# Planner numbers, PSUM bank pairs, two direct plane moves and halved steps in the prologue of a decoder layer kernel

## The reference, cut to what matters

```python
# x: (2, 1024, 256); ctx: (2, 77, 256)
K = 2 * Re(sum_n Ct[h,n] * exp(dtA[h,n] * l))            # S4D kernel, l = 0..1023
y = irfft(rfft(x, 2048) * rfft(K, 2048))[:1024]          # long convolution per channel
r = x + y + x * D
x = LN(x + LN(r) * ln_w + ln_b)                          # stage 1
x = LN(x + MHA(q=x, k=ctx, v=ctx))                       # 16 heads of 16, 77 keys
x = LN(x + MLP(x) + product_key_experts(x))              # 1024 wide MLP, 1024 experts
```

## Time and profile before

| what | us |
|---|---|
| median of three runs (689.98 to 695.78) | 693.98 |
| the profiled execution | 689.71 |
| its span in the trace | 687.9 |
| head up to the end of the last taps matmul | 0 to 119.4 |
| spectra, products, inverse | 119.4 to 165.8 |
| PE idle for the last planes | 165.8 to 176.9 |
| convolution, first norms, queries, to the first score subtraction | 176.9 to 201.2 |
| attention of the first tiles, with the other norms | 201.2 to 269 |
| attention and feed-forward | 269 to 688 |

### The profile page before, as it was taken

How to read it: one execution, slowest core, us unless ns; L and a number is a source line. 1 busy time by engine, 2 the same in 40 slices (tenths; PEclk the granted TensorE clock), 3 DMA queues, 4 the chain that set the end, 5 groups by cost and what they waited for, 6 DMA issues and landing times.

```text
span 687.9 us, 9791 instructions
## 1 busy us (share of the span) xinstructions
PE 599.0 (87%) x3200; PEld 393.4 (57%) x3200; DVE 484.3 (70%) x955; ACT 403.9 (59%) x595; POOL 308.5 (45%) x354
## 2 busy tenths in 40 slices
PE   6809588795769598999999999999999999899896
PEld 2503477573636364454776745578565478453485
DVE  7976475662346885897857789765779796678782
ACT  3865446222143265996673878773778774677760
POOL 3704975554142456352263632243735243744441
PEclk9858879899695677999999999999999999999999
DMA  8994020368161000000000000000000000000000
GB/s 272 309 235 90 1 76 27 101 171 224 27 247 59 1 1 1 0 2 0 1 0 1 17 8 9 0 1 1 8 16 1 9 1 1 9 15 9 0 9 23
DMA packets 19613, 34.14 MB, mean 50 GB/s; under 512 B 7273, under 2 KB 13931, under 8 KB 18219
## 3 DMA queue, kind: packets, MB, share of 16 engines
q1 hardware_dynamic: 15179, 29.33, 14.8%
q10 hardware_dynamic: 4384, 4.20, 1.9%
HBM read 21.81 MB, written 10.65 MB: 47 GB/s over the span
## 4 chain that ended last, share of the span: by engine, by line
PE 64%; DVE 12%; DMA 6%; ACT 6%; POOL 6%; issue 5%; SPq 1%; DVEq 0%; POOLq 0%; ACTq 0%
PE banks L804 20%; PE banks L894 8%; PE banks L899 8%; PE banks L849 4%; PE banks L871 4%; PE banks L826 3%; DMA scr_x<-arena 3%; PE banks L861 3%; PE banks L679 2%; PE banks L746 2%; PE banks L835 2%; DMA scr_v<-arena 2%; PE banks L886 2%; DVE stats L1437 2%; PE banks L716 1%
## 5 line engine op out<-in xcount | busy, mean ns | idle before, releaser
L1260 POOL TENSOR_TENSOR arena<-arena 128x1024 f32<-128x1024 f32 x64 | 123.3, 1927 | 159.1 <-ACT arena L1122 158.3
L804 PE MATMUL banks<-arena 128*128 128x512 f32 x384 | 174.4, 596 | 5.3 <-issue 3.7
L804 PEld LDWEIGHTS banks<-arena 128*128 128x128 f32 x384 | 69.8, 190 | 83.0 <-issue 76.9
L1122 ACT ACTIVATE arena<-arena 128x1024 f32<-128x1024 f32 x64 | 73.5, 1149 | 7.5 <-DVE arena L1525 3.0
L1124 ACT ACTIVATE arena<-arena 128x1024 f32<-128x1024 f32 x64 | 73.5, 1149 | 2.1
L1525 DVE SCALAR_TENSOR_TENSOR arena<-arena 128x1024 f32<-128x1024 f32 x48 | 63.9, 1331 | 1.7
L1012 ACT COPY arena<-banks 128x512 f32<-128x512 f32 (+1 forms) x64 | 34.1, 532 | 46.2 <-PE banks L796 30.3
L894 PE MATMUL banks<-arena 128*128 128x256 f32 x256 | 58.4, 381 | 2.4 <-DVE arena L1547 2.2
L1233 POOL TENSOR_SCALAR arena<-mv 128x1 f32<-128x1 f32 (+1 forms) x40 | 14.4, 361 | 102.1 <-DVE mv L1438 100.7
L899 PE MATMUL banks<-arena 128*128 128x256 f32 x256 | 57.9, 379 | 0.0
L1026 ACT ACTIVATE tok<-tok,arena,rstd 128x256 f32<-128x256 f32 x48 | 27.9, 598 | 44.0 <-POOL arena L1238 43.0
(11 more groups left out here) (179 smaller groups left out, 1096.3 us busy)
## 6 DMA issues: line engine op xcount, KB each, us to landing
scr_x<-arena SPq DMA_DIRECT2D x16, 256.0 KB, 8.9
arena<-scr_x SPq DMA_DIRECT2D x4, 1024.0 KB, 11.0
scr_z<-arena ACTq DMA_DIRECT2D x14, 256.0 KB, 3.8
tok<-in_x SPq DMA_DIRECT2D x8, 256.0 KB, 6.1
arena<-scr_z SPq DMA_DIRECT2D x4, 512.0 KB
out<-tok SPq DMA_DIRECT2D x16, 128.0 KB, 1.7
arena<-scr_z SPq DMA_DIRECT2D x2, 640.0 KB
arena<-in_imat SPq DMA_DIRECT2D x1, 1152.0 KB, 5.5
```

Of the source, the lines that this page charges most:

```text
L804: ins = mm(bk[:, :], w[:, k, P * m:P * m + P], src[:, k, :], start=(k == 0), stop=(k == KC - 1))
L1122: fn(ebuf[m % 2], sxb[m % 2], ACT.Prelu, bias=negt[:, n % 2, h:h + 1], alpha=FAR).then_inc(s_ranked, 1)
L1260: tt(sxb[m % 2], sim[:, n % 2, h, 0:XR].unsqueeze(2).broadcast_to((P, XR, NKEYS)), sim[:, n % 2, FH + h, :].unsqueeze(1).broadcast_to((P, ...
```

## The change

All of it lies before the steady part; the steps of the steady part keep their order.

* `x_bias` moves from between POOL's tables to behind all its `spectra`; `values` moves to between tables 7 and the second `skip`; `keys` on DVE to directly behind tables 7, ahead of `spectra`; ACT's `stage` behind `sines(1)`.
* `taps` and `x_second` are interleaved on PE and ACT, and the bank pair now alternates over the merged list (`PAIR_AT`). A step waits for the evacuation of the step two places before it in that list (`pair_free`). PE's and ACT's order becomes: x_second 0, 1, 2, taps 0, x_second 3, taps 1, x_second 4, 5, taps 2, x_second 6, taps 3, x_second 7, 8, taps 4, then (PE) k_first 0, taps 5, k_first 1, k_first 2, taps 6, k_first 3, taps 7. The steps x_second 0, 2, 3, 4, 8 and taps 2, 3, 5, 7 use banks 4 and 5, the others 0 and 1; so taps 0 and taps 1 share a pair.
* The last two planes' steps (n = 16 and 17, three planes) go from `zring` straight into `zB` by three moves of 128 KB inside SBUF, issued on ACT's queue; the second half has three batches left.
* `conv` is cut in two: for q = 0..5 the part of the first channel half runs as soon as the planes of that half are there and all evacuations of planes are done; q = 3, 4, 5 use banks 4, 0 and 1 for it (`CONV_APART`). q = 6, 7 run as before.
* The first group's queries are made in halves of 256 tokens: turn1 0, queries of half 0, score 0.0, conv 7, score 0.1, turn1 1, queries of half 1. ACT's order there: queries of half 0, norm1 1, conv 7, turn1 1, score 0.0's exponential, a query, score 0.1's exponential, a query. DVE takes score 0.0 and 0.1 back to back, and `ln` 3 ahead of `residual` 2.

```diff
-Z_BATCHES = ((0, 1, 2), (3, 4), (5, 6), (7, 8))
+Z_BATCHES = (((0, 1, 2), (3, 4), (5, 6), (7, 8)), ((0, 1, 2), (3, 4), (5, 6)))
+Z_DIRECT = (FREQ + 7, FREQ + 8)
+CONV_EARLY = (0, 1, 2, 3, 4, 5)
+CONV_APART = {3: 4, 4: 0, 5: 1}
...
+         "query_first": (-0.08, -0.07, 0.245, 0.2684), "score_first": (0.0, 0.043), "turn2": (-0.001, 0.0655),
-         "taps": (0.982,), "x_second": (-2.2, 0.237), "skip": (1.3, 0.3), "k_first": (5.915, 0.66, 9.6, 0.247),
-         "simw": (-2.4,), "x_bias": (-0.466, 0.617), "values": (-1.576,), "stage": (-2.515,), "keys": (9.738,),
+         "taps": (1.261,), "x_second": (-0.5, 0.7), "skip": (1.248, 0.3), "k_first": (5.915, 0.66, 9.6, 0.247),
+         "simw": (-2.4,), "x_bias": (12.0, 0.1), "values": (7.2,), "stage": (-2.151,), "keys": (7.496,),
...
+        PAIR_USERS = [y for y in order(HEAD, "pe") if y[0] in ("taps", "x_second")]
+        PAIR_AT = {y: i for i, y in enumerate(PAIR_USERS)}
...
+        def pair_bank(kind, n):
+            return 4 * ((PAIR_AT[kind, n] + 1) % 2)
+
+        def pair_free(kind, n):
+            at = PAIR_AT[kind, n]
+            if at < 2:
+                return (s_xae, 2 * NQ) if at else (s_kbz, 1)
+            last, k = PAIR_USERS[at - 2]
+            return (s_kev, 2 * k + 2) if last == "taps" else (s_xfe, k + 1)
...
-                if g >= 2:
-                    pe.wait_ge(s_kev, 2 * g - 2)
-                b0 = group_bank(g)
+                pe.wait_ge(*pair_free("taps", g))
+                b0 = pair_bank("taps", g)
...
-                    if n == 0:
-                        pe.wait_ge(s_kbz, 1)
-                        pe.wait_ge(s_xfe, FREQ)
                     taps(n)
...
+            def conv_part(q, hf):
+                bk = conv_bank(q)[:, :].rearrange("p (b f n) -> p f b n", b=B, f=2)
+                for h in range(2):
+                    ins = mm(bk[:, hf], fai[:, h, :], zB[:, hf, h, q, :].rearrange("p (b n) -> p b n", b=B),
+                             start=(h == 0), stop=(h == 1), skip_group_check=True)
+                return ins
...
+                pe.wait_ge(s_zr[1], 16 * z_loads(1))
+                if q not in CONV_EARLY:
+                    w_unit(("conv", q, "a"))
+                    conv_part(q, 0)
+                conv_part(q, 1).then_inc(s_wmm, 1)
+
+            pe.wait_ge(s_late, 16 * 4)
+            pe.wait_ge(s_kev, 2 * NGRP)
+            pe.wait_ge(s_kae, 2 * QUAD)
+            pe.wait_ge(s_cross, 2 * FREQ)
+            pe.wait_ge(s_ze, 2 * FREQ)
+            pe.wait_ge(s_zr[0], 16 * z_loads(0))
+            for q in CONV_EARLY:
+                conv_part(q, 0)
...
-                    act.dma_start(t["scr_z"][hf, tiles[0]:tiles[0] + planes].rearrange("r p n -> p r n"),
-                                  zring[:, d, 0:planes]).then_inc(s_zw[d], 16)
+                    if n in Z_DIRECT:
+                        for j, r in enumerate(tiles):
+                            act.dma_start(zB[NS * r:NS * r + NS, hf].rearrange("p h q n -> p (h q) n"),
+                                          zring[:, d, j, :]).then_inc(s_zr[hf], 16)
+                    else:
+                        act.dma_start(t["scr_z"][hf, tiles[0]:tiles[0] + planes].rearrange("r p n -> p r n"),
+                                      zring[:, d, 0:planes]).then_inc(s_zw[d], 16)
...
-                    fn(qT[:, j, :], src, ACT.Identity, bias=pcol[:, j:j + 1]).then_inc(s_wact, 1)
+                    fn(qT[:, j, query_cols(step)], src[:, query_cols(step)], ACT.Identity,
+                       bias=pcol[:, j:j + 1]).then_inc(s_wact, 1)
```

More of the change, by code:

```diff
@@ L55 @@
 PAIRS = [(0, NC)] + [(2 * m - 1, 2 * m) for m in range(1, FREQ - 1)] + [(NC - 1,)]
[L58 to L65, removed]
-         "taps": (0.982,), "x_second": (-2.2, 0.237), "skip": (1.3, 0.3), "k_first": (5.915, 0.66, 9.6, 0.247),
-         "simw": (-2.4,), "x_bias": (-0.466, 0.617), "values": (-1.576,), "stage": (-2.515,), "keys": (9.738,),
+PLACE = {"probs": (0.166, 0.2592, 0.441), "score": (0.273, 0.6341), "attend": (0.592,), "turno": (0.772,),
+         "project": (1.4,), "project_last": (0.934,), "turn1": (-0.087, 0.0432), "query": (0.245, 0.2685),
+         "query_first": (-0.08, -0.07, 0.245, 0.2684), "score_first": (0.0, 0.043), "turn2": (-0.001, 0.0655),
+         "sim": (0.379,), "sim_first": (0.031,), "best": (0.432,), "best_first": (0.207,),
+         "pair": (0.283, 0.3903, 0.7922, 0.8026), "total": (0.847,), "first": (-0.1,), "sums": (-0.805,),
+         "exps": (-0.131,), "late": (-0.027, 0.0082, 0.7012),
+         "conv": (-2.338, -1.7115, -1.497, -1.4195, -1.329, -1.2905, -1.172, -0.9595),
+         "ln": (-1.672, -1.4035, 0.316, 1.2245, 1.9406, 2.373, 3.035, 3.1435),
+         "ln_steps": (-0.501, -0.234, 0.162, 0.013, 0.361), "sines": (-2.943, -2.336), "tables": (0.152,),
+         "taps": (1.261,), "x_second": (-0.5, 0.7), "skip": (1.248, 0.3), "k_first": (5.915, 0.66, 9.6, 0.247),
+         "simw": (-2.4,), "x_bias": (12.0, 0.1), "values": (7.2,), "stage": (-2.151,), "keys": (7.496,),
@@ L119, in queries @@
             for j in range(2):
-                put(start, kind, s, j, j=j)
+                if kind == "query" and s == 0:
+                    for half in range(2):
+                        put(start, kind, s, j, half, key="query_first", j=2 * half + j)
+                else:
+                    put(start, kind, s, j, j=j)
     def normed(at, tl, k):
@@ L483, in build @@
                 key = step + (part_,)
+                if step[0] == "conv" and step[1] in CONV_APART:
+                    wide_count += 1
+                    CONV_DONE[step[1]] = (s_wmm, wide_count)
+                    continue
                 W_AT[key] = len(W_FREE)
@@ L497, in w_bank, with query_of, query_cols, conv_bank @@
             return bank[5 + u % 3]
+        def query_of(tl, hh):
+            return ("query", 0, hh, tl // 2) if tl < SUPER else ("query", tl // SUPER, hh)
+        def query_cols(step):
+            return slice(W // 2 * step[3], W // 2 * (step[3] + 1)) if step[1] == 0 else slice(0, W)
+        def conv_bank(q):
+            return bank[CONV_APART[q]] if q in CONV_APART else w_bank(W_AT[("conv", q, "a")])
         def spectrum_of_x(m, hf):
@@ L520, in taps_bank, with z_loads @@
             return bank[(4 if hf else 6) + g % 2]
+        def z_loads(hf):
+            return len(Z_BATCHES[hf]) + sum(len(tiles_of(n % FREQ)) for n in Z_DIRECT if n // FREQ == hf)
         def z_writes(upto, d):
@@ L610, in _ @@
             for hf in range(2):
-                for batch in Z_BATCHES:
+                for batch in Z_BATCHES[hf]:
                     for n in (FREQ * hf + k for k in batch):
@@ L616, in _ @@
                                  t["scr_z"][hf, r0:r1].rearrange("r (s c) n -> (r s) (c n)", s=NS)).then_inc(s_zr[hf], 16)
-            sp.wait_ge(s_wmm, max(W_DONE[W_AT[("conv", q, "a")]][1] for q in range(NQ)))
+            sp.wait_ge(s_wmm, max((CONV_DONE[q] if q in CONV_APART else W_DONE[W_AT[("conv", q, "a")]])[1] for q in range(NQ)))
             for dst, n in ((dn, "dn"), (wg, "wg"), (wu, "wu"), (wd, "wd"), (up, "up")):
@@ L842, in _ @@
                         pe.wait_ge(s_vbd, 1)
+                        pe.wait_ge(s_wact, max(ACT_TURN[("conv", q, "a")] for q in CONV_APART if CONV_APART[q] == 4))
                     for c in range(PCH):
@@ L910, in evac_taps @@
             g, half = divmod(i, 2)
[L911 removed]
+            src = bank[pair_bank("taps", g) + half][:, :].rearrange("p (k c) -> p c k", c=P)
             ch = CH * (g % HALF_GROUPS) + HC // 2 * half
```

52 lines of the change are left out of this document (18 added, 34 removed).

## The result

| what | us |
|---|---|
| kernel before, median of four runs (689.98 to 695.78) | 694.05 |
| changed kernel, median of four runs (670.55 to 673.4) | 671.67 |
| ratio, 95% interval | 0.9699 (0.9665 to 0.9734) |
| profiled executions, before and after | 689.71, 673.4 |
| their spans | 687.9, 671.6 |

The account below looks back on a forecast made before the run. Bound before 269 us by x's round trip, POOL's queue delaying taps 0, the planes' wait and serial first tiles; gains 15.0 + 0.5 + 10.5 = 26.0 off the 694.0 median gave 668.0 us, range 658 to 678.

Parts of the forecast that it names:

- The rival that the handovers are hidden: Tap groups: the tables pace the groups, not the handovers of banks; gain 32.4, time 661.6 us, chance 0.10.
- the clock rival: Tap groups: PE loses its clock between the mixed steps, costing 5.3; gain 20.7, time 673.3 us, chance 0.14.
- the rival that the head does nothing: Tap groups: something else than POOL holds taps 0; gain only 10.5, time 683.5 us, chance 0.03.
- the forecast's chain: Tap groups: taps 0 from 58.9, then waits for evacuations, taps 7 done at 104.5 instead of 119.45; gain 15.0.
- of 64 (groups 0 and 4) 4.26: Tap groups: price of a taps group of 64 matmuls at full clock, 4.26 us, against 2.13 for 32.
- the bound of 109: Tap groups: the forecast counts as wrong if taps 7 ends after 109 or before 100 us.
- Spectra: Phase of 46.4 us after the last taps: moving `keys` out of its middle gains 0.5, between 0 and 4.1.
- Planes: Before the convolution's second half: direct moves take 6.6, all planes there at 173.9 on the old axis, bounds 173.0 and 177.
- the bound of "no gain": Planes: upper bound on their arrival, 177 on the old axis, where the direct moves gain nothing.
- The rival of slow direct moves: Planes: at half rate three take 9.7, arriving at 177.2, no earlier than before; gain 22.7, time 671.3 us, chance 0.13.
- First tiles: Planes' arrival to DVE's first score: 17.5 instead of 24.3, gain 6.8; then a loss of 0.8 to the first `probs`.
- The better clock from `probs` on and the earlier `ln`: Behind the first `probs`: gain taken as 1.5, between nothing and 4 us for the clock and the `ln`.

Follow-up runs that it names:

- e2_pool_back: Changed kernel with `values` and `x_bias` put back at POOL's head, as before the change: 687.84 us, ratio to the kernel before 1.001.
- e5_keys_back: Changed kernel with `keys` put back between spectra 5 and 6 on DVE: 674.33 us, 1.75 above the changed kernel run beside it.
- e12_one_direct: Changed kernel with only the last plane moved directly and the two planes of step 16 sent through DRAM: 673.26 us.
- e6_conv_whole: Changed kernel with the convolution in one piece for all eight slices, without early parts: 671.57 us.
- e4_queries_whole: Changed kernel with the first group's queries in one piece each, behind both transposes: 680.62 us, ratio 0.987 to the kernel before.
- e9_taps_first: Changed kernel with x_second 7 and 8 moved behind all taps and k_first 0 to 3 given new places: 673.58 us.
- c1_after: The changed kernel run again without edits, as yardstick of the third set: 672.14 us, ratio 0.9738 to the kernel before.
- e1_planes_back: Changed kernel with the three direct plane moves undone, the last planes going through DRAM again: 670.10 us.

## Why the prediction was right or wrong

**Direction and mechanism of the head: right.** POOL's queue held taps 0; with it gone, taps follow the handovers of banks. POOL adds at 52.9 (forecast near 54), PE waits for ACT before taps 1 and 3, and e2_pool_back shows that nothing of the gain is left without it. The rival that the handovers are hidden is refuted by the waits of 1.0 to 1.5 us, the clock rival by the window of the whole stretch, in which the granted clock is 1.00, the higher of the two levels, with PE busy 43 of 52 us, and the rival that the head does nothing by 11.2 us.

```profile
60.00:112.00 52.00, 43.08 (x646) 32.56 (x644) 38.15 (x33) 34.55 (x82) 33.89 (x19) 1.00 0.22 60
```

**Its size: 15.0 was 11.2, a sum with four mis-sized terms.** Measured against the forecast's chain, the first taps began 1.1 us late (60.01 for 58.9; x's round trip ended 1.4 later in this execution, 52.38 against 50.98). The term "of 64 (groups 0 and 4) 4.26" was worked out by doubling 2.13; it is 5.03, twice on the chain, 1.5 us. The trace of before holds both such groups, partly at the lower clock (0.50 in 74 to 76, 0.76 over 95 to 102), and I had not read them:

```profile
71.71 6.57 PE L679 MATMUL banks<-arena 64*128 64x128 f32 x64 [2.56 <-POOL arena L1204]
...
95.36 6.59 PE L679 MATMUL banks<-arena 64*128 64x128 f32 x64 [2.11 <-DVE arena L1397]
```

From taps 3's end to taps 4's start it took 5.0 instead of 4.4: the chain had taps 4 start once x_second 7 was evacuated, but x_second 8 stands ahead of it on PE, waits for the evacuation of taps 3 and lasts 1.90. And the last v add took 2.91 for 2.35, 0.6. Smaller differences cancel; it makes 3.8: taps 7 end at 108.28 instead of 104.5, just inside the bound of 109.

**POOL and PE's order aren't additive.** I gave the 15 us to one chain and did not ask what each half gives alone. The runs do: 2.8 and -4.1 (in those two traces and the changed kernel's, x's trip ended 1.2 to 1.4 later than in that of before, so each could stand 1 us better).

**`keys` beside POOL: a cost that I left out.** I put `keys` under the last taps and priced only what it frees. It slows POOL there, and POOL slows it. A row of the kernel before showed it already, and I had not read it: beside `keys` at 134.29 POOL's products took 1.30 and 1.16, a little earlier 0.73.

```profile
133.45 0.73 POOL L1147 TENSOR_TENSOR arena<-arena 128x256 f32<-128x256 f32 x1
134.39 1.30 POOL L1146 TENSOR_TENSOR arena<-arena 128x256 f32<-128x256 f32 x1 [0.21 <-DVE arena L1413]
```

`keys` reads both operands from SBUF (`arena`, `head_mask`); the tables' products read one from PSUM (`banks`), and beside them POOL's adds keep 2.35. The Trainium skill (SBUF — State Buffer, SBUF: two separate sides) has the rule: a VectorE operation with two SBUF inputs and a GpSimd operation that reads SBUF share a pair of ports, which one of them holds for its whole instruction. The rows of `keys` agree with it in that both engines slow down (6.01 for `keys`, 4.08 for `values`, 2.91 for the add). They do not show that one waits the other out: from 102.98 to 108.99 work was done that alone takes about 8.0 us, by my estimate (4.13 of `keys`, 2.35 of the add, some 1.5 of `values`). No run here sets the ports apart from another cause.

**Spectra: 0.5 was 2.0.** I took PE for the bound because it was busy 8.19 of 9.00 us. All the same the stretch is 0.5 to 2.0 shorter in the ten traces with `keys` gone from it (e5_keys_back has the comparison).

**Planes: the step that failed.** "I take 6.6, and all planes are there" 6.7 us after the last evacuation; it was 11.8, beyond the 8 that I had set as the point where the forecast is wrong, and beyond the bound of "no gain". My nearest row was four moves that together took 4.55 and fill 32 partitions each; this move fills 8. The rival of slow direct moves held, which had the planes 10.0 us after the last evacuation; it is 1.8 more, so that they come later than through DRAM. The lower bound failed too: the last batch that SP reads was to land 4.87 after its issue, and took 10.86. The Trainium skill (DMA: Bandwidth & Descriptors, Why a DMA increments its semaphore by 16 and not by 1) had the sign: fewer of the 16 engines for such a shape. But half the rate is not the whole of it, since one move took as long as three (e12_one_direct): 12.0 us from the last evacuation for one, 11.8 for three. By the rival's own working, 9.7 for three, one would have taken 3.2.

**First tiles: 6.8 was 4.9, and 0.8 was 1.4.** Conv's second parts began at 1.2 GHz (granted clock 0.57 in 166 to 170, 1.00 from there on), behind 4.45 us in which PE did nothing (forecast under 3), and DVE's first statistics (169.19) came 2.8 us after the planes instead of 1.6. That is 1.2; the half queries took 3.7 for 3.4, and the transposes and copies ahead of them 0.4 more. That the queries would be at the lower level was right (0.50 over their 3.7 us). The early parts of conv, which I had counted with 1.4 us and as cover, are worth nothing (e6_conv_whole). The better clock from `probs` on and the earlier `ln`, which I had at 1.5 together, gave 2.2: `probs` takes 1.09 where it took 1.97. Without the halves the clock is lost, and they are worth 6 by the traces and 8 by the medians (e4_queries_whole).

**The level.** The sum was 26.0 against 16.2 in the traces, yet the time was only 3.7 off. That closeness is luck in good part, and comes from the two executions: before's profiled one lay 4.3 below its median, the changed kernel's 1.7 above. It is luck too that the slow moves' rival gave 671.3, next to the 671.67 measured: it had the planes 3.3 us later than the forecast, where they were 5.1 later, and nothing of the head's 3.8. The three medians' gains of 22.4, 19.4 and 18.0 say that the sum was too large by 4 to 8 us.

## What to carry to other kernels

When a queue's delay and another engine's order hide each other, price each edit alone as well as both: one of them can be a loss by itself. Before a round trip through DRAM is replaced by a move inside SBUF, look at how many partitions the move fills, and time one. Cutting a step in halves pays twice where PE would else wait, once on the path and once in the granted clock behind it; but filling PE's idle time in one place only moves the cold stretch unless it is filled up to the step on the path.

## What the runs showed of the hardware

* A group of 64 matmuls of 64x128 took 5.03, two groups of 32 of the same shape 2 x 2.13 = 4.26. In e9_taps_first 96 in a row took 6.86.
* DVE's multiplications for `keys` and POOL's operations beside them: 6.01 against 4.13, 4.08 against 2.71, 2.91 against 2.36 for the same instructions. Beside POOL's shorter products `keys` kept its 4.13, and they took 1.30 and 1.16 for 0.73.
* A move of 128 KB inside SBUF onto 8 partitions landed 11.23 us after its issue in c1_after. In the other traces with such moves the read of planes issued beside them took 9.3 to 11.3, whether one or three were issued; without them a write to DRAM and the read back took 4.79 + 4.57.
* Short idle pieces of PE were followed by the lower clock in one place and not in another. The early parts of conv, behind 2.20 us of idleness, were granted 0.54 and 0.50 in 156 to 158 and took 7.11 us, in e12_one_direct behind 1.23 us 5.42. The length of the pause does not decide it alone: behind 1.67 us they took 7.11 in e4_queries_whole, behind 1.73 us 5.42 in e2_pool_back; and in e1_planes_back the second parts began behind 2.14 us and took 7.17 at the full clock.
